# Macaron block with a Mamba-2 mixer, float32: the decays of the carried state by channel are fetched from stored sums of steps, in place of a matmul per mixer block

## The reference

```python
x = x + 0.5 * ffn(layernorm(x))
x = x + attn(layernorm(x))          # a Mamba-2 mixer
x = x + 0.5 * ffn(layernorm(x))

# the mixer, for 64 heads of 16 channels, a state of 128, chunks of 64 steps
gate, xBC, dt = split(x @ in_proj.T); xBC = silu(conv1d(xBC)); x, B, C = split(xBC)
dt = clip(softplus(dt + dt_bias), 0, 100); A = -exp(A_log)
A_cum = cumsum(A * dt, within a chunk)
Y_diag = (C B^T * L) (x dt)         # L = exp(segsum(A dt))
states = B (x dt) exp(A_cum[-1] - A_cum), carried from chunk to chunk
Y_off = (C states) * exp(A_cum)     # the decay of the carried state, by head and step
y = (Y_diag + Y_off + D x) * silu(gate); return rmsnorm(y) @ out_proj.T
```

## Time and profile before

| | |
|---|---|
| median of 3 timed runs | 1630.2 us (1630.0 to 1630.93) |
| the profiled execution, all of it | 1632.3 us |
| its span, first to last instruction | 1630.5 us |
| TensorE busy (matmuls) | 1607.1 us, 99% |
| VectorE, ScalarE, GpSimd busy | 1077.9, 661.6, 452.1 us |
| DMA, mean | 169 GB/s, 50.3% of the 16 engines' time |

### The profile page before, as it was taken

One profiled execution on the slowest core, in us unless ns is written; L12 is line 12 of the kernel. 1 busy time (PEld: TensorE's weight loads), 2 busy tenths in 40 slices (PEclk: granted clock), 3 DMA queues, 4 the chain that ended last, 5 costly groups with the idle time before them and its releaser, 6 DMA issues.

```text
span 1630.5 us, 25109 instructions
## 1 busy us (share of the span) xinstructions
PE 1607.1 (99%) x9612; PEld 1300.1 (80%) x9612; DVE 1077.9 (66%) x2051; ACT 661.6 (41%) x988; POOL 452.1 (28%) x362
## 2 busy tenths in 40 slices
PE   7999999999999999999999999999999999999999
PEld 4788888877888778888878888877888878778887
DVE  7544445776677877777777677777666676866543
ACT  5343434463333464333355333346343342343321
POOL 1656653011221212122112121221221222354400
PEclk9999999999999999999999999999999999999999
DMA  7855654754544454544535454545454446542334
GB/s 276 297 201 218 231 195 168 271 184 144 172 154 150 149 171 140 167 161 149 163 117 173 169 155 147 170 144 186 142 171 160 145 136 187 166 132 89 129 104 155
DMA packets 230887, 274.76 MB, mean 169 GB/s; under 512 B 14065, under 2 KB 190321, under 8 KB 222193
## 3 DMA queue, kind: packets, MB, share of 16 engines
q1 hardware_dynamic: 230768, 273.15, 50.3%
HBM read 222.79 MB, written 50.33 MB: 168 GB/s over the span
## 4 chain that ended last, share of the span: by engine, by line
PE 74%; DVE 3%; ACT 2%; issue 1%; DMA 0%; SPq 0%; ACTq 0%; DVEq 0%
PE bank L1274 24%; PE bank L1230 12%; PE bank L1320 11%; PE bank L1357 5%; PE bank L1455 5%; PE bank L1334 3%; PE bank L1524 3%; PE bank L1495 2%; PE bank L1511 2%; PE bank L1473 2%; PE bank L1483 1%; PE bank L1518 1%; DVE xT L2036 0%; PE bank L1258 0%; PE bank L1350 0%
## 5 line engine op out<-in xcount | busy, mean ns | idle before, releaser
L1274 PE MATMUL bank<-fxT,wj 128*128 128x512 f32 x1608 | 381.5, 390 | 0.0
L1274 PEld LDWEIGHTS bank<-fxT,wj 128*128 128x128 f32 x1608 | 301.6, 188 | 62.8
L1230 PE MATMUL bank<-xT,wi 128*128 128x512 f32 x900 | 222.9, 395 | 1.6 <-DVE m_cv L2154 0.5
L1320 PE MATMUL bank<-m_wd,m_hb 128*128 128x512 f32 x864 | 216.6, 393 | 1.0 <-DVE m_hb L2055 0.9
L1230 PEld LDWEIGHTS bank<-xT,wi 128*128 128x128 f32 x900 | 166.0, 188 | 39.7 <-issue 4.5
L1320 PEld LDWEIGHTS bank<-m_wd,m_hb 128*128 128x128 f32 x864 | 160.4, 188 | 35.0 <-issue 2.2
L1758 ACT CAST m_hb<-xn 128x512 fp32r<-128x512 f32 x76 | 47.1, 620 | 333.7 <-DVE xn L2049 325.9
L2525 POOL TENSOR_TENSOR m_L<-m_L,m_GT 128x512 f32<-128x512 f32 x36 | 52.8, 1466 | 431.7 <-ACT m_L L1808 431.7
L2062 DVE TENSOR_TENSOR res<-bank,res 128x512 f32<-128x512 f32 x148 | 102.0, 690 | 31.4 <-PE bank L1320 29.3
L1808 ACT ACTIVATE m_L<-bank 128x512 f32<-128x512 f32 x128 | 76.6, 599 | 84.0 <-PE bank L1473 83.7
L2049 DVE SCALAR_TENSOR_TENSOR xn<-bank,sc,xn 128x512 f32<-128x512 f32 x76 | 56.8, 747 | 69.9 <-PE bank L1274 68.9
(11 more groups left out here) (278 smaller groups left out, 2720.5 us busy)
## 6 DMA issues: line engine op xcount, KB each, us to landing
wj<-ug_split SPq DMA_DIRECT2D x155, 512.0 KB, 4.2
m_wd<-dn_split SPq DMA_DIRECT2D x43, 1024.0 KB, 5.0
wi<-in_split SPq DMA_DIRECT2D x76, 512.0 KB, 3.4
ug_split<-b_wu SPq DMA_DIRECT2D x8, 2048.0 KB, 13.1
m_wo<-out_split SPq DMA_DIRECT2D x32, 512.0 KB, 4.1
in_split<-b_msp SPq DMA_DIRECT2D x20, 512.0 KB, 3.9
wi<-ug_split SPq DMA_DIRECT2D x17, 512.0 KB, 4.1
raw<-in_wug SPq DMA_DIRECT2D x8, 1024.0 KB, 6.9
```

What stands on the lines that cost most here:

```text
L1230: ins = pe.matmul(to[:], w[:, a, k, :], xT[:, b, k, :], start=(k == 0 and i == 0), stop=(k == KH - 1 and i == 2))
L1274: ins = pe.matmul(to[:], w[:, a, k, :], frm[:, b, k, :], start=(k == 0 and i == 0), stop=(k == KH - 1 and i == 2))
L1320: ins = pe.matmul(down_bank(at, t)[:], hb[:, a, j, ck(t)], w[:, b, j, :], start=(j == 0 and n == 0), stop=(j == 1 and n == 2))
```

## The change

- `times_start`, `copies`, `i2r`, `i2x` and their semaphores are gone.
- `keep` stores the running sums of dt of 64 heads as well (`du[0:HEADS]` to `cum_d`, 128 KB), as the fifth store of a batch, and waits for five.
- `carried_sums(q, b)` on SP fetches the eight rows of a block, each repeated for 16 partitions, into `eb` (128 x 512, 256 KB). It waits for the exponential of the block before, since `eb` is one buffer, and stands behind `load_up(4 * at + 6)` of the block before; for block 0 behind `heads`.
- `times` takes exp(scale * eb) with the scale by partition `aex`, which is A spread over the channels of each block.
- `aex` is fetched at the start of the mixer: eight DMAs of 8 numbers of A_log, each repeated for 16 partitions, behind `load_up(3)`. ScalarE waits for all eight behind `step_exp(0)` and takes their exponential; VectorE negates it behind `sums_low(0)`.
- Waits on `s_ex` that stood for the bank X being read are now on `s_xd` (VectorE's product from X). `step_in` and `sums_high` wait on `s_kp`.

```diff
@@ keep, on SP
+                sp.wait_ge(s_eb, 16 * NB * (q + 1))
+                sp.dma_start(cum_d, du[0:HEADS, :]).then_inc(s_kp, 16)
                 if q == 0:
                     load_in(5)
-                sp.wait_ge(s_kp, 64 * q + 64)
+                sp.wait_ge(s_kp, 80 * q + 80)
+
+            def carried_sums(q, b):
+
+                wait(sp, s_ex, NB * q + b)
+                sp.dma_start(eb[:], cum_d[HPB * b:HPB * (b + 1), :].unsqueeze(1).to_broadcast([HPB, HDIM, SEQ])).then_inc(s_eb, 16)
@@ SP's order
             load_up(3)
+            for b in range(NB):
+                sp.dma_start(aex[:, b:b + 1], par[HPB * b:HPB * (b + 1), P_ALOG:P_ALOG + 1].unsqueeze(1).to_broadcast([HPB, HDIM, 1])).then_inc(s_eb, 16)
             load_in(4)
...
             heads(0, 0)
+            carried_sums(0, 0)
             load_in(6)
...
                     load_up(4 * at + 6)
+                    if not end:
+                        carried_sums(q, b + 1)
...
                     heads(q + 1, 0)
+                    carried_sums(q + 1, 0)
                     load_in(m0 + 2 * NB + 6)
@@ TensorE: x_rows (beside_turn and out_proj alike)
-                    pe.wait_ge(s_ex, NB * q + b)
+                    pe.wait_ge(s_xd, NB * q + b)
@@ TensorE
-            def times_start(q, b):
-
-                pe.wait_ge(s_ix, NB * q + b + 1)
-                pe.wait_ge(s_xd, NB * q + b + 1)
-                pe.matmul(X[:], i2x[:, b % 2, :], aS[:], start=True, stop=True).then_inc(s_E, 1)
...
-                    times_start(q, b)
@@ ScalarE, times
-                act.wait_ge(s_E, NB * q + b + 1)
+                act.wait_ge(s_eb, 16 * (NB * (q + 1) + b + 1))
+                if b == 0:
+                    act.wait_ge(s_ae, 2)
                 wait(act, s_yf, NB * q + b)
-                act.activation(ex[:], X[:], ACT.Exp).then_inc(s_ex, 1)
+                act.activation(ex[:], eb[:], ACT.Exp, scale=aex[:, b:b + 1]).then_inc(s_ex, 1)
@@ ScalarE, step_in and sums_high
+                wait(act, s_kp, 80 * q)
...
-                wait(act, s_E, NB * q)
+                wait(act, s_kp, 80 * q)
@@ ScalarE's order
             step_exp(0)
+            act.wait_ge(s_eb, 16 * NB)
+            act.activation(aex[:], aex[:], ACT.Exp).then_inc(s_ae, 1)
             raw(0, 0, NB)
@@ VectorE's order
             sums_low(0)
+            dve.wait_ge(s_ae, 1)
+            dve.tensor_scalar(aex[:], aex[:], -1.0, None, ALU.mult).then_inc(s_ae, 1)
@@ GpSimd
-            def copies(q, b):
-
-                wait(pool, s_E, NB * q + b - 1)
-                pool.tensor_copy(i2x[:, b % 2, :].rearrange("p (h d) -> p h d", d=HDIM),
-                                 i2r[:, HPB * b:HPB * (b + 1)].bitcast(F32).unsqueeze(2).to_broadcast([P, HPB, HDIM])).then_inc(s_ix, 1)
...
-                    copies(q, b)
```

More of the change, by code:

```diff
@@ L88, in program @@
     cum_m = nc.dram_tensor("cum_move", [NB, 2 * HPB, SEQ], F32, kind="Internal").ap()
+    cum_d = nc.dram_tensor("cum_step", [HEADS, SEQ], F32, kind="Internal").ap()
     cum_s = nc.dram_tensor("cum_stay", [2, SEQ // 64, HEADS, 64], F32, kind="Internal").ap()
@@ L96, in program @@
         acol = ctx.enter_context(nc.sbuf_tensor("acol", [P, 1], F32))
-        i2r = ctx.enter_context(nc.sbuf_tensor("i2r", [P, HEADS], F32R))
+        aex = ctx.enter_context(nc.sbuf_tensor("aex", [P, NB], F32))
         ones = ctx.enter_context(nc.sbuf_tensor("ones", [P, P], F32))
@@ L118, in program @@
         banks = [ctx.enter_context(nc.psum_tensor(f"bank{i}", [P, 512], F32)) for i in range(8)]
-        s = dict(res=res, cs=cs, pr=pr, sug=sug, sud=sud, acol=acol, i2r=i2r, ones=ones, xn=xn, banks=banks, raw=raw, draw=draw,
+        s = dict(res=res, cs=cs, pr=pr, sug=sug, sud=sud, acol=acol, aex=aex, ones=ones, xn=xn, banks=banks, raw=raw, draw=draw,
                  last=last, parts=parts, fxT=fxT, wi=wi, wj=wj, xT=xT, sc=sc, gate=gate, projected=projected, wi_full=wi_full, wj_full=wj_full)
         begin(nc, s, x, wug, wsc, wdn, win, wout, cst, par, ug_s, dn_s, in_s, out_s, mid_s)
-        mixer(nc, s, ug_s, dn_s, wsc, in_s, out_s, cum_m, cum_s, out)
+        mixer(nc, s, par, ug_s, dn_s, wsc, in_s, out_s, cum_m, cum_d, cum_s, out)
 def rsqrt(eng, ch, y, v, t, scale=1.0):
@@ L556, in _ @@
             pe.wait_ge(s_par, 64)
-            pe.wait_ge(s_c, 8)
+            pe.wait_ge(s_c, 7)
             group(0)
@@ L651, in _ @@
             act.activation(s["acol"][:], pr[:, P_ALOG:P_ALOG + 1], ACT.Exp).then_inc(s_ex, 1)
-            act.wait_ge(s_c, 8)
+            act.wait_ge(s_c, 7)
             group(0)
@@ L773, in _ @@
             dve.tensor_scalar(sud[:], pr[:, P_SUD:P_SUD + FB], 0.5 / math.sqrt(FF), None, ALU.mult).then_inc(s_c, 1)
-            dve.tensor_copy(s["i2r"][:], cs[:, C_I2:C_I2 + HEADS]).then_inc(s_c, 1)
             dve.tensor_copy(Hr[:], H).then_inc(s_c, 1)
-            dve.wait_ge(s_c, 6)
+            dve.wait_ge(s_c, 5)
             column = C_H + (PQ - 1) * FB
@@ L859, in _, with mixer @@
             add(n, (2, 3))
-def mixer(nc, s, ug_s, dn_s, wsc, in_s, out_s, cum_m, cum_s, out):
-    res, cs, pr, banks, ones, acol, i2r, xn, xT, fxT, win, wj, sc = (
-        s[n] for n in "res cs pr banks ones acol i2r xn xT fxT wi wj sc".split())
+def mixer(nc, s, par, ug_s, dn_s, wsc, in_s, out_s, cum_m, cum_d, cum_s, out):
+    res, cs, pr, banks, ones, acol, aex, xn, xT, fxT, win, wj, sc = (
+        s[n] for n in "res cs pr banks ones acol aex xn xT fxT wi wj sc".split())
     s_g, s_wi, s_wj, s_in = s["gate"], s["wi_full"], s["wj_full"], s["projected"]
@@ L928, in mixer @@
         rr = sb("rr", [P, 3 * TPG])
-        i2x = sb("i2x", [P, 2, P], F32R)
+        eb = sb("eb", [P, SEQ])
         (s_xn, s_tr, s_xhi, s_xlo, s_pev, s_rw, s_cv, s_xcv, s_e, s_ln, s_cu, s_ah, s_ce, s_xe, s_w,
          s_nu, s_dw, s_dt, s_as, s_dg, s_G, s_B, s_D, s_gt, s_bt, s_dd, s_X, s_xp, s_A, s_L,
-         s_xd, s_mv, s_mp, s_Y, s_S, s_st, s_O, s_E, s_ex, s_y, s_z, s_yf, s_ss, s_yh, s_yl, s_V, s_v,
-         s_op, s_oa, s_fin, s_own, s_po, s_z0, s_c0, s_sq, s_kp, s_ix, s_ld, s_wo, s_wd, s_out) = (sem(n) for n in (
+         s_xd, s_mv, s_mp, s_Y, s_S, s_st, s_O, s_ae, s_ex, s_y, s_z, s_yf, s_ss, s_yh, s_yl, s_V, s_v,
+         s_op, s_oa, s_fin, s_own, s_po, s_z0, s_c0, s_sq, s_kp, s_eb, s_ld, s_wo, s_wd, s_out) = (sem(n) for n in (
              "xn tr xhi xlo pev rw cv xcv e ln cu ah ce xe w nu dw dt as dg G B D gt bt dd X xp A L "
-             "xd mv mp Y S st O E ex y z yf ss yh yl V v op oa fin own po z0 c0 sq kp ix ld wo wd out").split())
+             "xd mv mp Y S st O ae ex y z yf ss yh yl V v op oa fin own po z0 c0 sq kp eb ld wo wd out").split())
         s_fxn, s_ftr, s_fxhi, s_fxlo, s_u, s_sil, s_h, s_hi, s_lo, s_d, s_acc = (
@@ L1255, in beside_turn @@
                 else:
-                    pe.wait_ge(s_ex, NB * mixed)
+                    pe.wait_ge(s_xd, NB * mixed)
                 for k in range(KH):
@@ L1436, in out_proj @@
                     pe.wait_ge(s_L, QUADS * MIXED)
-                    pe.wait_ge(s_ex, MIXED)
+                    pe.wait_ge(s_xd, MIXED)
                     pe.wait_ge(s_y, MIXED)
```

## The result

The changed kernel takes 1637.8 us (median of 5 runs, 1636.3 to 1638.4) where the kernel before takes 1630.9 (median of 5, 1630.0 to 1633.1) in the same session: 1.0038 times as long, 95% interval 1.0027 to 1.0050. It is slower by 0.4%, and 2.6 us above the upper end of the forecast's range. All five runs have a mean granted clock of TensorE of 0.996. The profiled execution is the fastest of the five, 1636.3 us, with a span of 1634.5.

What follows compares the result with a forecast made beforehand. The prediction took TensorE's own order of matmuls to bound the kernel. Slots -5.45, mixer start +4.75 and fifth store +1.05 sum to +0.35 us on 1630.2, forecast 1630.6 us, range 1626.0 to 1635.2.

Steps and rivals of the forecast that it cites:

- The slot: TensorE, per block: removing the times_start matmul frees 0.227 us in 24 of 32 blocks, 5.45 us gained.
- edits at nothing: GpSimd, VectorE, ScalarE: removed casts, added negation, exponential reading SBUF and changed waits cost no time.
- fetch per block: SP's queue, each block: the 256 KB fetch of carried sums has about 5 us of cover and costs zero.
- rival (5): Blocks: another wait, the exponential's for its fetch, replaces the slot, so no gain; 1636.0 us, chance 4%.
- rival (4): Blocks: a slot is worth 0.43 us in 31 blocks; 1622.7 us, chance 5%.
- The start of the mixer: ScalarE's wait for eight aex loads makes raw 6.0 us late; net cost 4.75 us (3.0 to 7.2).
- 1.25 us given back: Mixer start: earlier-cleared loads, VectorE's 0.32 us wait and TensorE's slack recover 1.25 us (0 to 2.1) of raw's delay.
- 0.9 us in hand: Mixer start: TensorE had 0.9 us of slack at ends_out, counted in the 1.25 us given back.
- rival (1): Mixer start: the idle stretch of about 5 us halves TensorE's clock, losing 1.9 us; 1632.5 us, chance 22% alone.
- The fifth store: keep, batches 1 to 3: heads waits for the added 128 KB store, 0.35 us each, 1.05 us in all.
- In batch 0 the emptier queues pay for it: keep in batch 0: the fifth store adds no cost of its own, the queues being emptier there.
- (2): Mixer start: aex loads cost 0.70 us each, 7.2 us stall, nothing given back; 1633.0 us, with rival (1) 1634.9; chance 12%.

Runs made afterwards that it cites:

- e4: The kernel before without the matmul times_start and GpSimd's casts, decays of the carried state left out of the result: 1627.0 us, ratio 0.9968.
- e8: e1 with the fifth store issued first in keep, and VectorE's first normalizing step of blocks 4 and 6 moved behind the convolution: 1627.9 us, ratio 0.9971.
- e11: e10 with VectorE's first normalizing step of blocks 4 and 6 moved behind states and the convolution: 1624.1 us, ratio 0.9953.
- e9: e3 with nine more useless matmuls ahead of from_states and two ahead of in_proj in block 0 of batch 0: 1632.5 us, ratio 1.0003.
- e10: The changed kernel with the eight aex loads issued at the end of begin, and heads not waiting for the fifth store: 1625.7 us, ratio 0.9966.
- e5: The kernel before with only the fifth store of keep added, for which heads waits: 1633.9 us, ratio 1.0007.
- e3: The changed kernel with 24 useless matmuls added ahead of ends_out(0): 1634.5 us, ratio 1.0015.
- e12: e5 with eight useless matmuls ahead of the first decay matmul of block 0 of batch 0: 1633.2 us, ratio 1.0015.
- e2: The kernel before with only the eight aex loads and ScalarE's wait and exponential added: 1641.6 us, ratio 1.0060.
- e1: The changed kernel with ScalarE's wait for aex and its exponential moved behind end_decays(0), VectorE's negation behind its conv: 1631.1 us, ratio 0.9994.

## Why the prediction was wrong

1. **The slot** was right. From block 1 of batch 0 to the end the changed kernel gains 4.9 us. The forecast for that stretch is 24 x 0.227 = 5.45 less the fifth store. In blocks 4 and 6 `in_proj` starts 0.59 to 0.60 us behind the start of the last matmul of `from_states` where it was 0.38 to 0.39, so the slot is lost there, as said. e4 confirms the sum, and e8 and e11 the reason.
2. **The edits at nothing and the fetch per block** were right. Nothing waits for the fetch, so rival (5) is out, and with a slot of 0.227 us rival (4) is too. Rival (5)'s 1636.0 us is nearer to the measured time than any other number of the prediction, by luck: its cause is not there.
3. **The start of the mixer** was right in place and kind, and short in size. A load of four-byte elements took 0.62 us of SP and not 0.55; `raw` was 6.5 us late and not 6.0. That is 0.5 us.
4. **"1.25 us given back"** failed. The wait for m_stn did fall, from 1.1 to 0.3 us (0.8 in e9), and TensorE's 5.5 us idle at `ends_out` against 6.5 is the 0.9 us in hand. But `from_states` then waits 2.1 us for VectorE; in the kernel before (waits of TensorE) that was

```profile
PE bank L1524 <- DVE m_sta L2200: 0.6, 1, 0.6
```

   so 1.5 us of it are taken back 12 us further on. I had named VectorE's chain as the next limit and given it only the 0.32 us of one wait. With no half clock (e9) the start costs 6.3 us at block 1, where the term said 4.75: 1.6 too little. Of the 6.5 us by which `raw` is late, 0.2 are given back, not 1.25.
5. **The clock**, rival (1), came in. The sum had it at nothing, and this is the largest error. It had 22% and a price of 1.9 us, taken from the 3.75 us of four slow matmuls at launch. Measured are two stretches of about 6.9 us, and 4.5 to 5.5 us of cost. Two steps failed: the length was read from one event of another kind, and a second wait behind the first was not considered as a second cause. The argument against it, that nothing in the mixer runs at half rate, spoke of a kernel without such a wait and should have had no weight. The Trainium skill's rule (TensorE: Matmul & The Clock Gate, HAM oscillation), that idle gaps send the array back to half clock, was right for the 5.5 us of idleness, where I made it the smaller case.
6. **The fifth store** was 0.35 us in each of batches 1 to 3; the distance from L1496 to L1486 grew by 0.42, 0.04 and 0.27 us, 0.7 in all for the forecast 1.05. In e4 and e10 that distance in batch 3 is over 1.1 us longer than in the kernel before, though nothing there waits for the store, so 0.7 us from one execution is rough. "In batch 0 the emptier queues pay for it" holds only in the changed kernel, where 6.5 us of delay cover it; in e5 the first decay matmul was 0.9 us later for it.

In the trace these sum up: -5.45 + 0.7 + 6.3 + 4.5 = +6.1 us, and the trace shows +6.0 at the end. (The 6.3 and 4.5 are cut out of the 10.9 at block 1 by e9, so only the other two are tested by this sum.) The time by medians is +6.8; the profiled execution, the shortest of five, is 4.0 up in its span because what precedes the mixer was 2 us shorter. Of the rivals whose cause was there, (1) and (2) together, 1634.9, came nearest, and still 2.9 us short.

## What to carry to other kernels

- Price the setup of an optimization as carefully as its steady part. 24 small gains of 0.23 us were worth 5 us, and one wait for eight 512-byte loads, put where an engine's chain has no gap, cost twice that. Issuing the same loads where the queue and the waiting engine are idle cost nothing.
- Where a change makes TensorE idle for longer than anything in its steady part, add the clock to the price, once for that wait and once more for the next one behind it. Filling each wait with useless matmuls told the two prices apart here (e3, e9); where the loss was small it didn't (e12).
- Read the granted clock of every timed run, of the kernel before too, ahead of building on one trace: half clock comes in some executions and not in others.
- Don't put a transfer under a semaphore that the critical queue waits on if only later work reads its data.

## What the runs showed of the hardware

- Waits of 5.5 us (changed kernel, e2) came in the profiles with about 6.9 us at 1.2 GHz, beginning at the end of the wait in the changed kernel and 2.6 us ahead of its end in e2, and all ten timed runs of the two have a clock of 0.995 to 0.997. Waits of 2.0 and 2.5 us (e5, e1) came with 3.4 us, in e5 not in every run: six of its eleven have 1.000. The wait of 1.1 us of the earlier trace rows came with none in that execution, but 34 of the kernel's 72 timed runs have a clock under 1.000.
- The profiles of the changed kernel, e1 and e5 had a second stretch as long as the first behind it, beginning 17 us after the first had ended in the changed kernel and 10 us after it in e1 and e5, beside waits of TensorE for VectorE (2.1 us at `from_states` in the changed kernel, 0.6 to 0.9 in e1 and e5). In e12, with the first wait filled, neither came; in e3, with the first wait filled, the second came all the same, behind a wait of 1.5 us. e10 and e11 have the same instructions and waits up to there (0.9 us at `from_states`), yet e10 had it and e11 had not. What decides is open.

```profile
366.00:371.00 5.00, 4.46 (x15) 3.49 (x14) 1.94 (x3) 0.63 (x1) 2.41 (x2) 0.66 0.00 0
```

```profile
366.00:372.00 6.00, 5.46 (x33) 4.67 (x33) 3.49 (x7) 1.61 (x3) 2.44 (x2) 1.00 0.01 1
```

- A load of 128 four-byte elements with a repeated source took SP 0.60 to 0.75 us to issue in the changed kernel, as long as a 128 KB store there (0.62), for 0.5 KB. In e1 one took 0.81 us, and in e10, at the end of `begin`, the first two took 1.3.
